# Moving three quarters of the key projections of a decoder layer from ahead of the loop into its first three steps, with the loads put in another order

## The chip, the cores and the metric

One core of one Trainium2 chip. The metric is the device time of one execution in microseconds (us), the median of several runs.

## The reference

A post-norm decoder layer over 32 batches of 128 tokens and 256 channels, all in float32:

```python
x = _layernorm(x + _L0_attn_ref(x, L0_attn_qkv_weights), axis=-1)      # 16 heads of 16, causal softmax
x = _layernorm(x + _L0_xattn_ref(x, ctx_1024, ctx_1024, ...), axis=-1)  # rotary q and k, decay mask, no softmax
x = _layernorm(x + _L0_ffn_ref(x, ...), axis=-1)                        # 8 experts, top 2, and a shared one
```

In the self-attention the keys are taken in an unusual way:

```python
q = jnp.transpose(pre_q, (0, 2, 1, 3)).reshape(-1, S, Dh)
k = jnp.transpose(pre_k, (0, 2, 3, 1)).reshape(-1, S, Dh)
a = jnp.einsum('aib,ajb->aij', q, k) / scale
```

The (channel, token) matrix of each head is read as (token, channel), so a row of k mixes 16 tokens of one channel. The kernel gets this order by a trip of the keys through device memory.

## The kernel before, in words

Five engines run programs of their own and meet on semaphores: TensorE (PE, `@block.tensor`), VectorE (DVE), ScalarE (ACT), GpSimd (POOL) and the DMA queue of SyncE (SP). The attention part is a software pipeline: `step(n)` on each engine handles scores of batch n, turns the probabilities of batch n-1, takes the heads of batch n-2, the cross attention of batches n-3 and n-4, the gate of batch n-5, and projects batch n+1 (`project`, q and v). The later parts (experts on gathered rows, the shared expert, the last norm) follow the loop and are not touched.

The keys go another way. The batches are in four groups of eight (`NG = 4`, `GB = 8`). `project_k(g, j, bank)` makes a quarter of a group's keys, called a tile here: tile i is quarter i % 4 of group i // 4. It is four float32 matmuls, eight in the profile, into one bank of PSUM (line 708). `out_k` (line 1238) copies the tile to SBUF on VectorE and counts `kk_set`. `store_k(g)` (line 445) waits for the group's four copies and stores 1 MB to `k_dram`. For each batch eight loads of 16 KB (line 480) bring its keys back as `kp`, in the order that `scores` (line 756) needs.

Order on TensorE before the loop: tiles 0 to 11 in banks 4 to 7, waits for all small tables and weights, then step -1 with `project(0)` and the first masks. Tiles 12 to 15 are inside: 12 and then 13 and 14 in step 0 behind its scores and its `project(1)`, tile 15 in step 1. The banks are used by others in the loop: 4 for turned probabilities, 5 for heads, 6 for q and v, 7 for the cross attention and the turned x1.

Order on SP before the loop: key weights, the four parts of x of group 0, x of groups 1 to 3 (1 MB each), identity, q and v weights, small loads (`load_small`, line 435: gate weights, biases, 705 KB of tables, the causal mask `tb`, cross attention weights), the store of group 0, then step by step: xT of batch n+2, kp of batch n+1, a store of another group at steps -1, 0 and 1, from step 3 to 6 the weights of the FFN (2.25 MB in the first of them, 1.5 MB in the others), ctx of batch n-2 and x of batch n-1. Each SP step begins with a wait for `project(n+1)` of TensorE (xT of two batches before must be free).

The masks (`lay_mask`, lines 1091 on ScalarE and 1359 on VectorE) write the causal mask of the next batch into the score banks once the exponentials have read them; scores(n+1) waits for all four.

Of the kernel before, what the change touches and what calls it, by code (L numbers as in the profile page):

```python
# [14 lines left out]
P = 128  # L15
# [17 lines left out]
GROUPS = [(lo, 4) for lo in range(0, B - 4, 4)] + [(B - 4, 2), (B - 2, 2)]  # L33
MAX_ORDER = (1, 0, 3, 2)
PADDING = B * S * TOPK
QB = 4
# [55 lines left out]
def decoder_kernel(nc, x, ctx_turned, wqkv, xwq, xwk, xwv, gate_w, gate_b, sw1, sb1, sw2, sb2,  # L92
                   rw1, rb1, rw2, rb2, table_f32, table_bf16, x_turned, x_blocks, out):
    ctx = ExitStack()
    with ctx:
# [196 lines left out]
        kk_set = sem("kk_set")  # L292
        k_stored = [sem("k_stored_first"), sem("k_stored_rest")]

# [110 lines left out]
        def live(t):  # L405
            return 0 <= t < B
# [15 lines left out]
        def _(eng):  # L422
            wqkv_rows = wqkv.rearrange("(c p) n -> p c n", p=P)
            eng.dma_start(wqkv_sb[:, :, D:2 * D], wqkv_rows[:, :, D:2 * D]).then_inc(wk_in, 16)
            for j in range(4):
                eng.dma_start(xTu[0][:, 2 * j:2 * j + 2, :, :, :].rearrange("p u c b i -> p (u c b i)"),
                              x_blocks[0, :, 2 * j:2 * j + 2].rearrange("p u n -> p (u n)")).then_inc(first_in[j], 16)
            for g in range(1, NG):
                eng.dma_start(xTu[g][:, :, :, :, :].rearrange("p u c b i -> p (u c b i)"),
                              x_blocks[g].rearrange("p u n -> p (u n)")).then_inc(xTu_in[g], 16)  # L430
            eng.dma_start(ident, table_f32[:, 0:P]).then_inc(ident_in, 16)
            for n in (0, 2):
                eng.dma_start(wqkv_sb[:, :, n * D:(n + 1) * D], wqkv_rows[:, :, n * D:(n + 1) * D]).then_inc(w_in, 16)

            def load_small():
                eng.dma_start(gate_w_sb[:, :, :], gate_w.rearrange("(c p) n -> p c n", p=P)).then_inc(small_in, 16)
                eng.dma_start(gate_b_sb[:, 0:NE], gate_b.rearrange("(o n) -> o n", o=1).broadcast_to([P, NE])).then_inc(small_in, 16)
                eng.dma_start(sb1_sb[:, :], sb1[0].rearrange("(c p) -> p c", p=P), allow_slow_non_contiguous=True).then_inc(small_in, 16)
                eng.dma_start(sb2_sb[:, :], sb2.broadcast_to([P, D])).then_inc(small_in, 16)
                eng.dma_start(tf[:, P:], table_f32[:, P:]).then_inc(tables_in, 16)  # L440
                eng.dma_start(tb[:, :], table_bf16).then_inc(tables_in, 16)
                for w, src in ((xwq_sb, xwq), (xwk_sb, xwk), (xwv_sb, xwv)):
                    eng.dma_start(w[:, :, :], src.rearrange("(c p) n -> p c n", p=P)).then_inc(xw_in, 16)

            def store_k(g):
                eng.wait_ge(kk_set, g * 4 + 4)
                eng.dma_start(k_dram[g * GB:(g + 1) * GB].rearrange("b i g f -> (b i) (g f)"),
                              kk_of(g)).then_inc(k_stored[min(g, 1)], 16)

            load_small()  # L450
            store_k(0)

# [13 lines left out]
            def step(n):  # L466
                t = n + 2
                if live(t):
                    after(eng, qv_made, t - 1)
                    eng.dma_start(xT[:, t % 2, :, :], x_turned[t]).then_inc(xT_in[t % 2], 16)  # L470
                t = n + 1
                if live(t):
                    after(eng, scored, (t - 1) * 4)
                    if t < 2:
                        eng.wait_ge(consts_set, 2)
                    if t == 0:
                        eng.wait_ge(k_stored[0], 16)
                    for j in range(GB):
                        lo = 16 * j
                        eng.dma_start(kp[lo:lo + DH, t % 2, j % 2, :, :].rearrange("p a u -> p (a u)"),  # L480
                                      k_dram[t, :, j, :]).then_inc(kp_in[t % 2], 16)
                if n in (-1, 0, 1):
                    store_k(n + 2)
                if n == 3:
                    eng.wait_ge(k_stored[1], 16 * (NG - 1))
                if 2 < n <= 2 + NE // 2:
                    if n == 3:
# [3 lines left out]
                    for e in range(2 * (n - 3), 2 * (n - 2)):  # L491
# [11 lines left out]
                if live(t):  # L503
                    after(eng, res1_set, t - 1)
                    eng.dma_start(xn[:, t % 2, :], x[t]).then_inc(xn_in[t % 2], 16)
                if n == B:
                    eng.wait_ge(qv_made, B)
# [196 lines left out]
        def _(eng):  # L704
# [8 lines left out]

            for g in range(NG - 1):
                eng.wait_ge(xTu_in[g] if g else wk_in, 16)
                for j in range(4):
                    if g == 0:
                        eng.wait_ge(first_in[j], 16)
                    else:
                        eng.wait_ge(kk_set, (g - 1) * 4 + j + 1)  # L720
                    project_k(g, j, 4 + j)
            eng.wait_ge(xTu_in[NG - 1], 16)
            eng.wait_ge(ident_in, 16)
            eng.wait_ge(w_in, 32)
            eng.wait_ge(kk_set, 4 * NG - 5)
            eng.wait_ge(tables_in, 32)
            eng.wait_ge(xw_in, 48)
            eng.wait_ge(small_in, 64)
            eng.wait_ge(consts_set, 2)

            def project(t):
# [96 lines left out]

            def step(n):
                if n == 1:  # L830
                    eng.wait_ge(kk_set, 13)
                if live(n - 1):
                    turn_probs(n - 1, 0)
                if n == 2:
                    eng.wait_ge(kk_set, 4 * NG)
                if live(n - 2):
# [3 lines left out]
                if n == 0:  # L840
                    eng.wait_ge(kk_set, 9)
                    project_k(NG - 1, 0, 4)
                if n == 1:
                    eng.wait_ge(kk_set, 14)
                    project_k(NG - 1, 3, 5)
                t = n - 3
# [20 lines left out]
                if live(n - 1):  # L867
                    turn_probs(n - 1, 1)
                t = n - 3
                if live(t):  # L870
# [23 lines left out]
                if live(n - 1):  # L894
                    turn_probs(n - 1, 2)
                t = n - 5
                if live(t):
# [31 lines left out]
                if n == 0:  # L929
                    eng.wait_ge(kk_set, 12)  # L930
                    project_k(NG - 1, 1, 5)
                    project_k(NG - 1, 2, 7)
                for q in groups_at(n, 3):
# [15 lines left out]
                if live(t):  # L949

                    eng.wait_ge(x1_set, t + 1)
                    after(eng, gc_set, n - 4)
# [282 lines left out]
        def _(eng):  # L1235
            def out_k(g, j, bank):
                eng.wait_ge(k_made, g * 4 + j + 1)
                eng.tensor_copy(kk_of(g).rearrange("p (a u) -> p u a", u=NU)[:, 2 * j:2 * j + 2, :],
                                ps[:, bank, :].rearrange("p (u a) -> p u a", u=2)).then_inc(kk_set, 1)

            for g in range(NG - 1):
                for j in range(4):
                    out_k(g, j, 4 + j)
            eng.wait_ge(tables_in, 32)
            eng.wait_ge(consts_set, 2)
            eng.tensor_copy(base[:, :], region_rows).then_inc(base_set, 1)

            eng.tensor_copy(zeros[:, D:PACKET], padding_end).then_inc(zeros_set, 1)

# [111 lines left out]
            def step(n):  # L1361
                t2, t3, t4, t5 = n - 2, n - 3, n - 4, n - 5
                r2, r4 = t2 % 2, t4 % 2
                if live(n):
                    for u in MAX_ORDER[:3]:
# [3 lines left out]
                if n == 0:  # L1369
                    for j, bank in enumerate((4, 5, 7)):  # L1370
                        out_k(NG - 1, j, bank)
                if n == 1:
                    out_k(NG - 1, 3, 5)
                if live(t2):
# [279 lines left out]
```

## Time and profile before

| | us |
|---|---|
| median of 3 runs | 769.59 |
| lowest, highest | 768.74, 775.72 |
| the profiled execution | 775.48 |
| its span | 773.6 |

The span is that from the first to the last instruction in the trace; the rest of the profiled execution's time lies around it. The mean granted TensorE clock of the span is 0.967 of full speed.

### The profile page before, as it was taken

What the parts mean: (1) busy time and instruction counts of PE and PEld (TensorE: products, weight loads), DVE (VectorE), ACT (ScalarE), POOL (GpSimd) and SP (SyncE); (2) the same over time, 40 slices, a digit from 0 to 9 for tenths busy, and PEclk for the clock granted to TensorE, in tenths of its full rate; (3) what the DMA queues carried; (4) which work ended last, traced back from release to release, by engine and by line L of the source; (5) the groups of instructions that cost most, each with busy time, mean ns of one, the idle gap of its engine ahead of it and who ended that gap; (6) DMA issues with size and microseconds to landing.
All of it is one profiled execution on the core that took longest, in us unless ns stands there. A gap on an engine that the chain in (4) does not pass through costs nothing.

```text
span 773.6 us, 19404 instructions
## 1 busy us (share of the span) xinstructions
PE 705.6 (91%) x5464; PEld 533.1 (69%) x5465; DVE 499.1 (65%) x1568; ACT 410.3 (53%) x1167; POOL 319.1 (41%) x451
## 2 busy tenths in 40 slices
PE   6978899999999999999987639999999999999993
PEld 6857788888888888888875315666666666665453
DVE  3555678888988888898866432444444444438985
ACT  0268688888888888888851102333333333312233
POOL 1001233335554554455455542555555555541111
PEclk9999999999999999999999677999999999999998
DMA  8644462213332332333271432422222222229962
GB/s 290 253 145 157 138 223 74 83 57 106 102 97 82 103 109 77 100 101 108 85 228 62 151 124 88 152 83 88 83 87 89 82 89 84 86 61 320 302 215 81
DMA packets 77032, 97.54 MB, mean 126 GB/s; under 512 B 12320, under 2 KB 63264, under 8 KB 75936
## 3 DMA queue, kind: packets, MB, share of 16 engines
q1 hardware_dynamic: 59920, 68.21, 28.0%
q0 software_dynamic: 6816, 19.00, 6.8%
q10 hardware_dynamic: 10224, 9.42, 4.4%
q8 instruction: 39, 0.64, 0.3%
q14 instruction: 33, 0.27, 0.1%
HBM read 60.02 MB, written 36.56 MB: 125 GB/s over the span
## 4 chain that ended last, share of the span: by engine, by line
PE 67%; issue 14%; DVE 5%; SPq 5%; DMA 4%; POOL 2%; ACT 1%; POOLq 0%; ACTq 0%; DVEq 0%
PE ps L990 16%; PE ps L1001 8%; PE ps L777 5%; PE ps L765 4%; PE ps L855 4%; PE ps L742 4%; PE ps L787 4%; PE ps L879 3%; PE ps L745 3%; PE ps L858 3%; PE ps L976 2%; PE ps L983 2%; DMA attn_only<-in_ctx 2%; DVE products L1263 2%; PE ps L865 2%
## 5 line engine op out<-in xcount | busy, mean ns | idle before, releaser
L1079 ACT ACTIVATE prob<-ps,nmax 128x128 f32<-128x128 f32 x512 | 146.8, 378 | 30.2 <-DVE nmax L1253 30.2
L990 PE MATMUL ps<-first_use,xgT 128*128 x284 | 137.3, 607 | 1.3 <-ACT xgT L1184 1.2
L1486 DVE TENSOR_TENSOR hid<-ps,attn_only 128x512 f32<-128x512 f32 x71 | 49.1, 692 | 93.8 <-PE ps L990 93.8
L1184 ACT COPY xgT<-ps 128x256 f32<-128x256 f32 x71 | 26.5, 373 | 133.9 <-PE ps L976 131.7
L1253 DVE TENSOR_REDUCE nmax<-ps 128x4 f32<-128x512 f32 x128 | 82.2, 685 | 22.7 <-PE ps L765 21.0
L671 POOL TENSOR_TENSOR gate_h<-hid,sil 128x256 f32<-128x256 f32 x71 | 50.9, 717 | 100.3 <-DVE result_row L1499 82.7
L1086 ACT COPY pT<-ps 128x512 f32<-128x512 f32 x128 | 76.7, 599 | 19.2 <-PE ps L777 14.5
L621 POOL TENSOR_TENSOR rot<-products 128x128 f32<-128x128 f32 x128 | 61.2, 499 | 60.9 <-DVE products L1263 57.8
L777 PE MATMUL ps<-tf,prob 128*128 128x128 f32 x512 | 78.6, 276 | 5.8 <-ACT pT L1086 5.7
L990 PEld LDWEIGHTS ps<-first_use,xgT 128*128 128x128 f32 x284 | 54.7, 194 | 41.1 <-issue 37.5
L640 POOL DMA_INDIRECT sent<-packets,pos x64 | 63.6, 994 | 37.1 <-PE ps L765 22.8
L674 POOL DMA_INDIRECT back<-yg,result_row x71 | 71.8, 1011 | 13.8 <-issue 12.3
L1001 PE MATMUL ps<-first_use,ghT 128*128 x284 | 74.0, 383 | 0.5 <-ACT ghT L1189 0.5
L777 PEld LDWEIGHTS ps<-tf,prob 128*128 128x128 f32 x512 | 59.3, 141 | 11.7 <-issue 5.4
L795 PE MATMUL ps<-prob,sw_sb 128*128 128x512 f32 x128 | 62.5, 639 | 3.9 <-DMA prob<-x2T_dram 2.7
L976 PEld LDWEIGHTS ps<-tf,xg 128*128 128x128 f32 x142 | 19.1, 144 | 54.9 <-issue 54.2
L1505 DVE TENSOR_TENSOR yg<-ps,attn_only 128x256 f32<-128x256 f32 x71 | 30.2, 425 | 39.3 <-PE ps L1001 36.7
L1001 PEld LDWEIGHTS ps<-first_use,ghT 128*128 128x128 f32 x284 | 48.3, 190 | 4.9 <-issue 0.9
L1263 DVE TENSOR_TENSOR products<-ps,tf 128x256 f32<-128x256 f32 x128 | 46.3, 404 | 6.0 <-PE ps L879 2.0
L795 PEld LDWEIGHTS ps<-prob,sw_sb 128*128 128x128 f32 x128 | 25.5, 203 | 33.4 <-issue 29.2
L653 POOL TENSOR_TENSOR rstd<-mv,neg_half 128x1 f32<-128x1 f32 x32 | 17.7, 552 | 67.5 <-DVE mv L1271 67.5
L1359 DVE CAST ps<-tb 128x512 f32<-128x512 bf16 x62 | 42.0, 682 | 2.1 <-ACT prob L1079 2.1
(135 smaller groups left out, 1390.2 us busy)
## 6 DMA issues: line engine op xcount, KB each, us to landing
xg<-sent ACTq DMA_DIRECT2D x68, 129.5 KB
first_use<-back SPq DMA_DIRECT2D x8, 1024.0 KB, 8.2
k_dram<-first_use SPq DMA_DIRECT2D x4, 1024.0 KB, 4.3
attn_only<-in_x_turned SPq DMA_DIRECT2D x32, 128.0 KB, 2.7
attn_only<-k_dram SPq DMA_DIRECT2D x256, 16.0 KB
attn_only<-in_x SPq DMA_DIRECT2D x32, 128.0 KB, 2.6
attn_only<-in_ctx SPq DMA_DIRECT2D x32, 128.0 KB, 2.6
first_use<-in_L_ffn_rw SPq DMA_DIRECT2D x8, 512.0 KB, 5.0
```

Of the source, the lines that this page charges most:

```text
L621: eng.tensor_tensor(rot[:, t % 2, m + e, :], ra[:, t % 2, m + e, :], rb[:, t % 2, m + 1 - e, :], ALU.add).then_inc(done, 1)
L640: eng.indirect_dma_start(sent, bass.IndirectOffsetOnAxis(ap=pos[:, t, j:j + 1], axis=0), packets[:, t % SLOTS, :], None).then_inc(sent_in[ ...
L671: eng.tensor_tensor(gate_h[:, r, :], hid[:, r, FFN:2 * FFN], sil[:, r, :], ALU.mult).then_inc(gh_set, 1)
L674: eng.indirect_dma_start(back, bass.IndirectOffsetOnAxis(ap=result_row[:, slot:slot + 1], axis=0), yg[:, slot % 2, :], None).then_inc(yg_o ...
L777: mm = eng.transpose(PROBT[:, n * P:(n + 1) * P], prob[:, t % 2, 4 * u + n, :], ident)
L795: mm = eng.matmul(ps[:, bank0 + 2 * f + half, :].rearrange("p (b t) -> p b t", b=QB), sw1_sb[:, c, cols:cols + P], x2T4[:, r, :, c, :], st ...
L990: mm = eng.matmul(ps[:, r, :], xgT[:, r, c, :], rw1_sb[:, bass.ds(e * (DC * 2 * FFN) + c * 2 * FFN, 2 * FFN)], start=(c == 0), stop=(c == ...
L1001: mm = eng.matmul(ps[:, 4 + r, 0:D], ghT[:, r, c, :], rw2_sb[:, bass.ds(e * (FFN // P * D) + c * D, D)], start=(c == 0), stop=(c == FFN // ...
L1079: ins = eng.activation(prob[:, t % 2, 4 * u + n, :], SCORE[u][:, n * P:(n + 1) * P], ACT.Exp, bias=nmax[:, t % 2, 4 * u + n:4 * u + n + 1])
L1086: eng.copy(pT[:, u, :, :].rearrange("p n t -> p (n t)"), PROBT).then_inc(pT_set, 1)
L1253: eng.tensor_reduce(nmax[:, t % 2, 4 * u:4 * u + 4], SCORE[u].rearrange("p (h j) -> p h j", j=P), AX_X, ALU.max, negate=True).then_inc(max ...
L1263: eng.tensor_tensor(into[:, t % 2, m:m + 2, :], source, table[:, m:m + 2, :], ALU.mult).then_inc(done, 1)
```

## The change

Tiles 0 to 3 are projected ahead of the loop and copied there. Tiles 4 to 15 move: 4, 5 and 6 to the head of step 0 ahead of its scores, 7 and 8 behind scores(0), 9 and 10 behind `project(1)`; 11 behind scores(1), 12 and 13 behind the second and third turn of the probabilities in step 1; 14 behind scores(2) and 15 behind the third turn of step 2. `K_BANK` names each tile's bank; a tile waits until the one before it in the same bank has been copied. The copies on VectorE move along, in program order. The base and zeros copies of VectorE move from ahead of the loop to step 1.

The loads have a new order: q and v weights, xT of batches 0 and 1, the mask (with a semaphore of its own) and the identity go in front; then x of group 1, the small loads, x of groups 2 and 3. The store of group 0 is split: batch 0 (16 partitions, 128 KB) and the rest, each with its semaphore; batch 0's kp waits for the first alone. The other stores come at the end of SP's steps 0, 1 and 2 instead of in the middle of -1, 0 and 1, and the FFN weights at steps 4 to 7 instead of 3 to 6. TensorE's waits for tables, cross attention weights and small loads move to the steps that use them.

```diff
+K_BANK = (4, 5, 6, 7, 4, 5, 7, 4, 5, 7, 5, 7, 5, 7, 7, 7)
@@ SP
-            for g in range(1, NG):
+            for n in (0, 2):
+                eng.dma_start(wqkv_sb[:, :, n * D:(n + 1) * D], wqkv_rows[:, :, n * D:(n + 1) * D]).then_inc(w_in, 16)
+            for t in range(2):
+                eng.dma_start(xT[:, t, :, :], x_turned[t]).then_inc(xT_in[t], 16)
+            eng.dma_start(tb[:, :], table_bf16).then_inc(mask_in, 16)
+            eng.dma_start(ident, table_f32[:, 0:P]).then_inc(ident_in, 16)
+
+            def load_blocks(g):
                 eng.dma_start(xTu[g][:, :, :, :, :].rearrange("p u c b i -> p (u c b i)"),
                               x_blocks[g].rearrange("p u n -> p (u n)")).then_inc(xTu_in[g], 16)
-            eng.dma_start(ident, table_f32[:, 0:P]).then_inc(ident_in, 16)
-            for n in (0, 2):
-                eng.dma_start(wqkv_sb[:, :, n * D:(n + 1) * D], wqkv_rows[:, :, n * D:(n + 1) * D]).then_inc(w_in, 16)
...
             def store_k(g):
                 eng.wait_ge(kk_set, g * 4 + 4)
-                eng.dma_start(k_dram[g * GB:(g + 1) * GB].rearrange("b i g f -> (b i) (g f)"),
-                              kk_of(g)).then_inc(k_stored[min(g, 1)], 16)
-
+                rows = k_dram[g * GB:(g + 1) * GB].rearrange("b i g f -> (b i) (g f)")
+                if g == 0:
+                    eng.dma_start(rows[0:DH, :], kk_of(g)[0:DH, :]).then_inc(k_stored[0], 16)
+                    eng.dma_start(rows[DH:P, :], kk_of(g)[DH:P, :]).then_inc(k_stored[1], 16)
+                else:
+                    eng.dma_start(rows, kk_of(g)).then_inc(k_stored[2], 16)
+
+            load_blocks(1)
             load_small()
+            for g in range(2, NG):
+                load_blocks(g)
             store_k(0)
@@ SP, step
-                if live(t):
+                if live(t) and t > 1:
                     after(eng, qv_made, t - 1)
                     eng.dma_start(xT[:, t % 2, :, :], x_turned[t]).then_inc(xT_in[t % 2], 16)
...
-                    if t == 0:
-                        eng.wait_ge(k_stored[0], 16)
+                    if t < 2:
+                        eng.wait_ge(k_stored[t], 16)
...
-                if n in (-1, 0, 1):
-                    store_k(n + 2)
-                if n == 3:
-                    eng.wait_ge(k_stored[1], 16 * (NG - 1))
-                if 2 < n <= 2 + NE // 2:
+                if n == 4:
+                    eng.wait_ge(k_stored[2], 16 * (NG - 1))
+                if 3 < n <= 3 + NE // 2:
...
+                if n in (0, 1, 2):
+                    store_k(n + 1)
@@ TensorE
-            for g in range(NG - 1):
-                ...
-                    project_k(g, j, 4 + j)
+            def project_ks(first, end):
+
+                for i in range(first, end):
+                    if i == 0:
+                        eng.wait_ge(wk_in, 16)
+                    if i < 4:
+                        eng.wait_ge(first_in[i], 16)
+                    elif i % 4 == 0:
+                        eng.wait_ge(xTu_in[i // 4], 16)
+                    if K_BANK[i] in K_BANK[:i]:
+                        eng.wait_ge(kk_set, i - K_BANK[:i][::-1].index(K_BANK[i]))
+                    project_k(i // 4, i % 4, K_BANK[i])
+
+            project_ks(0, 4)
             eng.wait_ge(w_in, 32)
+            eng.wait_ge(mask_in, 16)
             eng.wait_ge(consts_set, 2)
+            eng.wait_ge(kk_set, 3)
@@ VectorE, step
+                if n == 0:
+                    out_ks(4, 7)
+                    eng.wait_ge(mask_in, 16)
+                    eng.wait_ge(consts_set, 2)
                 if live(n):
                     for u in MAX_ORDER[:3]:
                         maxes(n, u)
                     if n < 2:
                         maxes(n, MAX_ORDER[3])
                 if n == 0:
-                    for j, bank in enumerate((4, 5, 7)):
-                        out_k(NG - 1, j, bank)
+                    out_ks(7, 11)
                 if n == 1:
-                    out_k(NG - 1, 3, 5)
+                    out_ks(11, 14)
+                    eng.wait_ge(tables_in, 16)
+                    eng.tensor_copy(base[:, :], region_rows).then_inc(base_set, 1)
+                    eng.tensor_copy(zeros[:, D:PACKET], padding_end).then_inc(zeros_set, 1)
+                if n == 2:
+                    out_ks(14, 16)
```

## Rows read from the trace of the kernel before

**Rows 1.** The page, busy time of TensorE and of VectorE over the span.

```profile
PE 705.6 (91%) x5464; PEld 533.1 (69%) x5465; DVE 499.1 (65%) x1568; ACT 410.3 (53%) x1167; POOL 319.1 (41%) x451
```

**Rows 2.** Chain of waits up to scores(1): start us, us, what.

```profile
18.63 8.60 DMA k_dram<-first_use
...
30.46 1.62 DMA attn_only<-k_dram
...
32.22 1.17 PE ps L765 x32
33.39 1.92 PE ps L708 x8
35.32 0.89 PE ps L742 x8
36.21 0.87 PE ps L745 x4
37.07 3.47 PE ps L708 x16
...
40.56 1.08 DVE first_use L1238
41.65 1.19 DVE ps L1359 x2
```

**Rows 3.** Chain of waits, steps 1 and 3: start us, us, what.

```profile
43.08 1.70 PE ps L765 x32
44.78 3.02 PE ps L708 x8
47.80 0.45 PE ps L777 x4
...
48.28 0.59 ACT pT L1086
48.87 0.14 issue
...
54.23 1.18 PE ps L765 x32
...
71.78 7.96 DMA attn_only<-in_ctx
```

**Rows 4.** DMA view of the first 32 us: GB/s in 40 slices of 0.8 us.

```profile
GB/s 0 0 55 365 156 146 246 315 379 410 417 420 461 399 451 410 410 412 337 365 179 123 193 315 338 390 378 433 424 424 387 278 129 47 8 30 32 39 40 188
```

**Rows 5.** Source view of the stores of keys (line 447), 0 to 80 us.

```profile
DMA to landing us min/median/max: 4.2/4.3/8.6
```

**Rows 6.** Windows: stretch, us, busy of each engine, granted clock, DMA share, GB/s.

```profile
44.00:46.00 2.00, 2.00 (x19) 1.59 (x15) 1.21 (x3) 0.48 (x2) 0.00 (x0) 0.50 0.13 33
46.00:48.00 2.00, 2.00 (x10) 1.62 (x9) 1.44 (x4) 1.70 (x7) 0.00 (x0) 0.76 0.00 0
...
65.95:76.53 10.58, 9.50 (x123) 8.34 (x119) 7.16 (x17) 9.20 (x28) 2.41 (x5) 1.00 0.68 217
76.53:91.38 14.85, 12.33 (x129) 10.50 (x125) 8.44 (x23) 9.40 (x28) 3.03 (x6) 0.89 0.56 184
91.38:102.50 11.12, 10.92 (x136) 9.79 (x132) 8.75 (x25) 9.58 (x29) 3.76 (x7) 1.00 0.59 189
```

**Rows 7.** Timeline of TensorE: start us, us, instructions [idle before them and its releaser].

```profile
43.08 1.70 PE L765 MATMUL ps<-attn_only 32*128 32x128 f32 x32 [2.12 <-DVE ps L1359]
...
58.92 0.63 PE L777 MATMUL ps<-tf,prob 128*128 128x128 f32 x4 [2.34 <-ACT pT L1086]
...
79.79 1.16 PE L855 MATMUL ps<-attn_only 128*128 128x128 f32 x8 [2.09 <-DMA attn_only<-in_ctx]
```

**Rows 8.** Timeline of VectorE, columns as in rows 7.

```profile
14.82 1.08 DVE L1238 COPY first_use<-ps 128x512 f32<-128x512 f32 x1 [0.65 <-PE ps L708]
...
57.20 0.25 DVE L1376 RECIPROCAL rden<-ps 128x16 f32<-128x16 f32 x1
...
59.16 0.69 DVE L1253 TENSOR_REDUCE nmax<-ps 128x4 f32<-128x512 f32 x1
```

More of the change, by code:

```diff
@@ L292, in decoder_kernel @@
         kk_set = sem("kk_set")
-        k_stored = [sem("k_stored_first"), sem("k_stored_rest")]
+        k_stored = [sem("k_stored_batch"), sem("k_stored_group"), sem("k_stored_rest")]
+        mask_in = sem("mask_in")
         xT_in = [sem("xT_in0"), sem("xT_in1")]
@@ L481, in step @@
                                       k_dram[t, :, j, :]).then_inc(kp_in[t % 2], 16)
-                if n in (-1, 0, 1):
-                    store_k(n + 2)
-                if n == 3:
-                    eng.wait_ge(k_stored[1], 16 * (NG - 1))
-                if 2 < n <= 2 + NE // 2:
-                    if n == 3:
+                if n == 4:
+                    eng.wait_ge(k_stored[2], 16 * (NG - 1))
+                if 3 < n <= 3 + NE // 2:
+                    if n == 4:
                         eng.dma_start(sw1_sb[:, :, :], sw1[0].rearrange("(c p) n -> p c n", p=P)).then_inc(ffn_in, 16)
                         eng.dma_start(sw2_sb[:, :, :], sw2[0].rearrange("(c p) n -> p c n", p=P)).then_inc(ffn_in, 16)
-                    for e in range(2 * (n - 3), 2 * (n - 2)):
+                    for e in range(2 * (n - 4), 2 * (n - 3)):
                         lo = e * DC * 2 * FFN
@@ L712, in project_k @@
                 mm.then_inc(k_made, 1)
-            for g in range(NG - 1):
[L715 to L720, printed above, removed]
-                    project_k(g, j, 4 + j)
-            eng.wait_ge(xTu_in[NG - 1], 16)
-            eng.wait_ge(ident_in, 16)
+            def project_ks(first, end):
[10 more added lines that the diff above has]
+            project_ks(0, 4)
             eng.wait_ge(w_in, 32)
[L725 to L728, printed above, removed]
+            eng.wait_ge(mask_in, 16)
             eng.wait_ge(consts_set, 2)
+            eng.wait_ge(kk_set, 3)
             def project(t):
@@ L829, in step @@
             def step(n):
+                if n == 0:
+                    project_ks(4, 7)
                 if n == 1:
-                    eng.wait_ge(kk_set, 13)
+                    eng.wait_ge(ident_in, 16)
+                    eng.wait_ge(kk_set, 8)
+                if n == 3:
+                    eng.wait_ge(tables_in, 16)
+                    eng.wait_ge(xw_in, 48)
+                if n == 5:
+                    eng.wait_ge(small_in, 64)
                 if live(n - 1):
@@ L834, in step @@
                 if n == 2:
-                    eng.wait_ge(kk_set, 4 * NG)
+                    eng.wait_ge(kk_set, 13)
                 if live(n - 2):
@@ L840, in step @@
                 if n == 0:
-                    eng.wait_ge(kk_set, 9)
-                    project_k(NG - 1, 0, 4)
+                    project_ks(7, 9)
                 if n == 1:
-                    eng.wait_ge(kk_set, 14)
-                    project_k(NG - 1, 3, 5)
+                    project_ks(11, 12)
+                if n == 2:
+                    project_ks(14, 15)
                 t = n - 3
@@ L868, in step @@
                     turn_probs(n - 1, 1)
+                if n == 1:
+                    project_ks(12, 13)
                 t = n - 3
@@ L895, in step @@
                     turn_probs(n - 1, 2)
+                if n == 1:
+                    project_ks(13, 14)
+                if n == 2:
+                    project_ks(15, 16)
                 t = n - 5
@@ L929, in step @@
                 if n == 0:
-                    eng.wait_ge(kk_set, 12)
-                    project_k(NG - 1, 1, 5)
-                    project_k(NG - 1, 2, 7)
+                    project_ks(9, 11)
                 for q in groups_at(n, 3):
@@ L951, in step @@
                     eng.wait_ge(x1_set, t + 1)
+                    if n == 2:
+                        eng.wait_ge(kk_set, 4 * NG)
                     after(eng, gc_set, n - 4)
@@ L1235, in _, with out_ks @@
         def _(eng):
[L1236 to L1248, printed above, removed]
+            def out_ks(first, end):
+                for i in range(first, end):
+                    eng.wait_ge(k_made, i + 1)
+                    eng.tensor_copy(kk_of(i // 4).rearrange("p (a u) -> p u a", u=NU)[:, i % 4 * 2:i % 4 * 2 + 2, :],
+                                    ps[:, K_BANK[i], :].rearrange("p (u a) -> p u a", u=2)).then_inc(kk_set, 1)
+            out_ks(0, 4)
             def maxes(t, u):
@@ L1363, in step @@
                 r2, r4 = t2 % 2, t4 % 2
+                if n == 0:
+                    out_ks(4, 7)
+                    eng.wait_ge(mask_in, 16)
+                    eng.wait_ge(consts_set, 2)
                 if live(n):
@@ L1369, in step @@
                 if n == 0:
-                    for j, bank in enumerate((4, 5, 7)):
-                        out_k(NG - 1, j, bank)
+                    out_ks(7, 11)
                 if n == 1:
-                    out_k(NG - 1, 3, 5)
+                    out_ks(11, 14)
+                    eng.wait_ge(tables_in, 16)
+                    eng.tensor_copy(base[:, :], region_rows).then_inc(base_set, 1)
+                    eng.tensor_copy(zeros[:, D:PACKET], padding_end).then_inc(zeros_set, 1)
+                if n == 2:
+                    out_ks(14, 16)
                 if live(t2):
```

1 line of the change is left out of this document (removed).

## The prediction

> **What bounds the kernel now.** The page comes first: TensorE is busy for 91% of the span and no other engine for more than 65% [rows 1]. So TensorE's order of work sets the time, and an edit is worth what it takes from or adds to TensorE's path. The change acts only on the first steps, so the next view is the chain of waits over the first 60 us. It runs through the DMA queue, not through TensorE, until 32.22: store of the first group's keys (lands 27.23), eight loads of batch 0's padded keys, and only then scores(0) at 32.22 [rows 2]. All twelve projections that stand ahead of the loop lie beside that DMA work and cost nothing. From 32.22 on the chain is TensorE with short hand-overs. I use the start of scores(n) (line 765) as the clock of the steps: 32.22, 43.08, 54.23 [rows 2, 3], then 65.95, 76.53, 91.38, 102.5 [rows 6]. The third view is the DMA rate by slices of 0.8 us [rows 4], for what a transfer is queued behind. The fourth is the granted clock [rows 6]: it is 0.50 in 44 to 46, after TensorE had stood still for 2.1 us [rows 7]. The fifth is the order of TensorE and VectorE in step 2 [rows 7, 8].
>
> **The start.** The store of group 0 is still issued after every load. Bytes ahead of it, counted from the shapes: 6.83 MB before, 7.09 MB after, since the two xT loads now stand ahead of it. Summing the slices of [rows 4], 6.83 MB have passed at 22.4 us and the store's 1.05 MB at 24.6; it lands at 27.23, 2.6 later. After: 7.09 MB have passed at 23.1, batch 0's 0.13 MB at 23.4, so it lands between 25.3 and 26.0; I take 25.6, a gain of 1.6. From landing to scores(0) was 32.22 - 27.23 = 4.99 (eight issues, the last one's landing of 1.62 [rows 2]) and is the same again. Scores(0) then starts at about 30.6. Bounds: no gain, if the small store lands with its sibling; and 3.0, if it lands 1.2 sooner still. The keys themselves are no limit: the fourth copy is done at 15.9 [rows 8]. The Trainium skill, "DMA: Bandwidth & Descriptors", Rules for kernel authors, says of two transfers to disjoint partition halves "Don't bother — they serialize". By that rule the split would be worth nothing in bytes; what I count is only that the first part's own semaphore fires earlier, and the slices agree that bytes go in order (8.60 us for the queued store against a median of 4.3 [rows 2, 5]).
>
> **What moves into the loop.** Before, 12 of 16 tiles (a tile is one project_k) come ahead of the loop and 4 inside steps 0 and 1. After, 4 come ahead, 3 (tiles 4 to 6) between the first masks and scores(0), where TensorE waits for the keys anyway, and 9 inside steps 0 to 2 behind a scores. That is five tiles more on the path side. A warm tile is 3.47 / 2 = 1.73 us [rows 2], so 8.7 us more work. The cover is what TensorE idles in these steps.
>
> Ahead of scores(0): TensorE works on 7 tiles, project(0) and the masks and ends near 22, then waits over 8 us. Before, it came to scores(0) after under 1 us of idling at full clock. The nearest row for a start after a wait is scores(1): 1.70 instead of 1.17 for the scores and 3.02 instead of 1.92 for the tile behind it, at a granted clock of 0.50, which is the 1.2 GHz level [rows 2, 3, 6]. The Trainium skill, "TensorE: Matmul & The Clock Gate", Part 1, also has TensorE fall to the lower of two clocks when idle; a wait of 8 us would then be answered by these same cold rows.
>
> Step 0: scores 1.70, tile 7 cold 3.02, tile 8 1.73, project(1) 0.89 + 0.87 = 1.76, tiles 9 and 10 3.47, then as before VectorE's copy of the last tile 1.08, two masks 1.19, hand-overs 0.27: 14.2. Before it was 10.86. So **+3.4**. Bounds: +1.7 if TensorE were warm, the bare extra tile; +6.5 if it stayed cold for the whole step (further tiles at 3.02, project(1) at twice its time less the overlap).
>
> Step 1: scores(1) follows again a 2.1 us wait for VectorE's masks, so 1.70 and 3.02 stay. Tiles 12 and 13 now stand between the turns of the probabilities, where TensorE waited 0.02 + 0.59 + 0.14 = 0.75 for ScalarE twice [rows 3]. So 2 x (1.73 - 0.75) less the slower turns = 1.6: the step goes from 11.15 to 12.7, **+1.6**. VectorE's four maxima, three copies and its base and zeros copies end before scores(2) needs its masks; ScalarE's last pT, exponentials, mask and q copy end 0.5 before the TensorE work does. Nobody else is late.
>
> Step 2: tile 14 falls into the idle time ahead of the turn at 58.92 [rows 7] (2.3 us long, so it is free). Tile 15 stands between the third and the fourth turn. VectorE does its copy, by program order, before the reciprocal, res1, the last maximum and x1. Before, the reciprocal began at 57.20, 2.97 after scores(2). After, tile 15 ends 4.69 + 0.44 + 1.73 = 6.86 after scores(2), its copy at 7.96, and the maximum 1.96 later [rows 8] at 9.9. Then ScalarE's four exponentials (1.15), x1T, mask and q copy end at about 13.2, against the 11.7 of before. TensorE has nothing to do from about 9.1 to 11.2 (2.1 us, waiting for x1), so comes out cold, and its transposes, turns and weigh end at about 14.1. I take 14.1 against 11.7: **+2.3**, bound +1.5 if it stays warm. The slow rows after scores(1) span 4.7 us [rows 3]; the same stretch here reaches into step 3: **+1.0**, or 0.
>
> Queues: SP now waits for kk_set 8, 12 and 16 at the end of its steps 0 to 2, in front of xT and kp of the next step. It gets them at 36.5, about 50.7 and s2 + 8; the next entry waits for project(1), (2) and (3), which end later each time. So the stores cost nothing there. POOL's zeros for the idle rows go out near 55 instead of 30.5; no load that is soon due stands behind.
>
> Step 5: the weights of the FFN are issued one step later, so the wait for ctx moves from step 4 to step 5. There it was 79.79 - 77.70 = 2.09 plus a cold stretch; step 4 took 14.85 against 11.12 of step 5, an excess of 3.7 [rows 6, 7]. The ctx issued behind 2.25 MB landed 7.96 after its issue at 71.78 [rows 3], 13.8 after scores(3). Steps 4 and later are 11.1 long instead of step 3's 10.58, so the same landing leaves a wait of 13.8 - 12.3 = 1.5. **-1.0**; bounds -2.2 (0.6 less wait and no cold stretch) and 0.
>
> **Sum** on the profiled execution of 775.5 (span 773.6 and 1.9 around it): -1.6 + 3.4 + 1.6 + 2.3 + 1.0 - 1.0 = +5.7, so 781.2 there. That execution lies 5.9 above the median of 769.6, inside the spread of the three runs (768.7 to 775.7); the difference carries over: **775.3**. From scores(6) on nothing differs.
>
> **Rivals.** (a) *The clock stays up*, because tiles fill TensorE's gaps. Deciding place: scores(0) and the tiles behind it at 1.17 and under 2. Step 0 then +1.7, step 1 -0.2 (1.70 and 3.02 become 1.17 and 1.73), step 2 +1.5, step 3 nothing, step 5 -2.2, start -1.6: -0.8, **768.8**, not slower. For it: idle stretches of 0.77 and 0.95 left the clock alone. Against: 2.1 us didn't, and the new wait is over 8. 0.12.
> (b) *The small store overtakes the loads.* Its place is the queue: if it lands about 2.7 after its issue instead of behind 7 MB, and SP's long issues go with the lighter queue, scores(0) starts near 23.6, -8.6 instead of -1.6; the sum is -1.3, **768.3**. It decides if k_stored fires before about 20. Against it is the 8.60 of [rows 2]. 0.05.
> (c) *TensorE stays cold through step 0 and part of step 1.* The wait before it is four times any seen here. Step 0 +6.5, one more tile of step 1 cold +1.3: +10, about **779.7**, slower by over 1%. 0.22.
> (d) The forecast, 0.61.
>
> **From this to the numbers.** About 1% (7.7 us) is what this kernel's measurement tells from no change, given the spread above. The forecast's own bounds run from about 771 to 779. The range takes in (a) and most of (c): 768.5 to 779.5, with some 2 in 10 outside. Slower by over 1% means above 777.3: (c) and a little of (d), 0.24. Faster by over 1% means below 761.9, which no case reaches: 0.02. The rest is 0.74.
>
> **What the changed profile would show.** Scores(0) at 30 to 31; 1.70 and about 3.0 for it and the tile behind; 14.2, 12.7 and 14.1 from scores to scores; tile 15's copy directly ahead of the reciprocal in step 2; the wait for ctx in step 5, near 1.5; 11.1 for step 4. It would be wrong if the first store lands at another time than 25 to 26, or if the clock answers the long wait otherwise.

## The result, and the profile after

The changed kernel takes 775.16 us (median of 20 runs), the kernel before 770.31 (20 runs). The ratio is 1.0067, 95% interval [1.0045, 1.0088]: 5.2 us slower, between 3.5 and 6.8. The ratio leaves out three slow runs of the changed kernel (one of them took 934.7 us at a granted clock of 0.834), so it does not quite match the two medians, which are 4.9 us apart. The forecast was 775.3. A second series of the same kernel gave 1.0070 [1.0029, 1.0110] (the run after_again).

The chain of waits of the profiled execution (span 772.9) up to step 5: start us, us, what. It answers to [rows 2, 3].

```profile
15.55 11.17 DMA k_dram<-first_use
...
29.92 1.62 DMA attn_only<-k_dram
31.54 0.14 issue
31.68 2.09 PE ps L779 x32
33.77 4.80 PE ps L720 x16
38.57 0.89 PE ps L756 x8
39.46 0.86 PE ps L759 x4
40.32 3.47 PE ps L720 x16
43.79 0.02 issue
43.81 1.08 DVE first_use L1267
44.90 1.19 DVE ps L1381 x2
46.08 0.28 issue
46.36 2.09 PE ps L779 x32
48.45 2.56 PE ps L720 x8
...
58.99 1.18 PE ps L779 x32
...
89.10 7.41 DMA attn_only<-in_ctx
```

The windows of the steps, from scores to scores; it answers to [rows 6]. Columns: stretch, us, busy time of PE, PEld, DVE, ACT and POOL, granted clock, DMA share, GB/s.

```profile
31.68:46.36 14.68, 12.53 (x81) 10.80 (x81) 8.00 (x10) 6.59 (x21) 0.00 (x0) 0.85 0.34 115
46.36:58.92 12.56, 12.56 (x117) 10.91 (x117) 6.99 (x11) 7.68 (x23) 1.15 (x1) 0.87 0.24 92
58.92:72.00 13.08, 10.34 (x119) 8.69 (x115) 7.97 (x15) 8.78 (x26) 0.58 (x1) 1.00 0.64 201
72.00:82.57 10.57, 9.50 (x122) 8.33 (x118) 7.16 (x17) 9.23 (x28) 2.41 (x5) 1.00 0.16 45
82.57:93.60 11.03, 10.71 (x129) 9.12 (x125) 8.45 (x23) 9.30 (x28) 3.01 (x6) 1.00 0.61 191
93.60:106.60 13.00, 11.01 (x134) 9.82 (x131) 8.78 (x25) 9.56 (x29) 3.77 (x7) 1.00 0.71 225
```

The timeline of TensorE at its longest waits, which answers to [rows 7], and that of VectorE in step 2, which answers to [rows 8]:

```profile
31.68 2.09 PE L779 MATMUL ps<-attn_only 32*128 32x128 f32 x32 [9.47 <-DMA attn_only<-k_dram]
...
70.18 0.44 PE L982 MATMUL ps<-tf,x 128*128 128x128 f32 x2 [1.95 <-DVE x L1438]
...
96.56 1.16 PE L877 MATMUL ps<-attn_only 128*128 128x128 f32 x8 [1.78 <-DMA attn_only<-in_ctx]
```

```profile
66.07 1.09 DVE L1267 COPY first_use<-ps 128x512 f32<-128x512 f32 x1 [2.92 <-PE ps L720]
67.00 0.22 DVE L1406 RECIPROCAL rden<-ps 128x16 f32<-128x16 f32 x1
...
68.93 0.69 DVE L1275 TENSOR_REDUCE nmax<-ps 128x4 f32<-128x512 f32 x1
```

Line 779 is scores, 720 a tile, 877 the first matmul on ctx, 1267 a tile's copy. The reader is to see: scores(0) starts only 0.54 us sooner (31.68), after a wait of 9.47; step 0 is 3.8 longer than before, step 1 1.5, step 2 1.3, step 3 the same, step 4 3.8 shorter (the wait for ctx has left it) and step 5 1.9 longer (it has come here). Scores(8) starts at 129.03, before at 125.26: +3.8. From scores(8) to scores(31) every profile of this study shows 257.2 to 257.8, so what the change does is over at scores(8), and I use that mark for each kernel. The spans of the two profiled executions (773.6 and 772.9) do not show the difference: that of before lost 2.6 us more between scores(31) and the first expert tile, and 2 more in the experts, in work that the change does not touch. The mark has its own spread: a second profile of before has it at 129.66, a second one of the changed kernel at 130.99 (the runs before_again and after_again), so one profile against one shows where time goes, and not the total.

| start of scores, us | 0 | 1 | 2 | 3 | 4 | 5 | 6 | 8 |
|---|---|---|---|---|---|---|---|---|
| before | 32.22 | 43.08 | 54.16 | 65.95 | 76.53 | 91.38 | 102.49 | 125.26 |
| after | 31.68 | 46.36 | 58.92 | 72.00 | 82.57 | 93.60 | 106.60 | 129.03 |
| after_again | 31.80 | 47.20 | 59.84 | 73.80 | 85.04 | 96.06 | 108.52 | 130.99 |
| before_again | 36.86 | 50.59 | 60.46 | 72.24 | 82.82 | 95.18 | 106.30 | 129.66 |

### The profile page after: what moved, and what is told of

Its sections match the earlier page's. It is cut to its first block, busy times and chain, and to the rows that moved or that the text cites. A ratio compares the mean times of both kernels' runs of the same rounds, so it can differ in the third digit from the quotient of the medians.

```text
span 772.9 us, 19407 instructions
## 1 busy us (share of the span) xinstructions
PE 700.9 (91%) x5464; PEld 530.8 (69%) x5465; DVE 498.8 (65%) x1568; ACT 410.4 (53%) x1167; POOL 318.6 (41%) x451
## 4 chain that ended last, share of the span: by engine, by line
PE 70%; issue 14%; DVE 5%; POOL 4%; DMA 4%; SPq 1%; ACT 1%; POOLq 0%; ACTq 0%; DVEq 0%
PE ps L1018 16%; PE ps L1029 8%; PE ps L791 5%; PE ps L779 5%; PE ps L877 4%; PE ps L801 4%; PE ps L756 4%; PE ps L880 3%; PE ps L903 3%; PE ps L759 3%; PE ps L720 3%; PE ps L1004 2%; POOL sent L652 2%; PE ps L1011 2%; DVE products L1285 2%
## 5 line engine op out<-in xcount | busy, mean ns | idle before, releaser
L1018 PE MATMUL ps<-first_use,xgT 128*128 x284 | 135.6, 600 | 1.5 <-ACT xgT L1212 1.5
L779 PE MATMUL ps<-attn_only 32*128 32x128 f32 x1024 | 39.4, 292 | 11.6 <-DMA attn_only<-k_dram 9.5
L665 POOL TENSOR_TENSOR rstd<-mv,neg_half 128x1 f32<-128x1 f32 x32 | 17.6, 550 | 68.4 <-DVE mv L1293 68.4
```

Of the source, the lines that this page charges most:

```text
L779: mm = eng.matmul(SCORE[u][:, n * P:(n + 1) * P].rearrange("p (d u) -> p d u", u=NU), qT[32 * u:32 * u + 32, t % 2, c, :], kp[32 * u:32 * ...
L1018: mm = eng.matmul(ps[:, r, :], xgT[:, r, c, :], rw1_sb[:, bass.ds(e * (DC * 2 * FFN) + c * 2 * FFN, 2 * FFN)], start=(c == 0), stop=(c == ...
```

## The experiments

All ratios are against the kernel before, run on the same chip beside them; one profile each. The median of the kernel before was 770.31 to 773.52 us in the different series, so ratios, and not times, are to be compared between experiments. Where the start of scores(8) is given as sooner or later, it is against the first profile of the kernel named.

**1. Loads alone** (loads_only): the kernel before with the new load order and the split store; tiles, stores of groups 1 to 3 and FFN weights as before.

> The kernel before with the new order of loads and the split store, and the tiles where they were. Theory (the moved tiles cost, the loads do not): scores(0) starts at 31.7 to 32.0 instead of 32.22, the steps are those of before (10.9, 11.1, 11.8), the time is within 0.2% of before. Rival (the order of loads costs by itself, as group 2's x now lands late and holds tiles 8 to 11 and with them project(0)): scores(0) after 33, 0.2 to 0.5% slower. Rival of the other sign (the loads bring what was to be had and only the tiles hide it): 30.6 and 0.2% faster.

Measured: 771.69 us, ratio 0.9992 [0.9972, 1.0013]. In its profile scores(0) starts at 33.30: the x of group 2 lands late (its load ends the wait of TensorE at 23.5) and tiles 8 to 11, project(0) and the masks follow it. Steps 0 and 1 are 10.86 and 11.14. Step 2 is 10.12 instead of 11.79, and step 4 is 17.60 instead of 14.85, with a wait of 3.88 for ctx, so the theory's "steps of before" did not hold there, and scores(8) is at 127.51 (+2.3). So the place of scores(0) is what the first rival said, its price in the time is not seen, and the loads alone neither pay nor gain: the 0.67% comes with the rest of the change, the tiles above all.

**2. Tiles alone** (tiles_only): the changed kernel with the loads in the old order and the store in one piece.

> The changed kernel with the loads in the order of before and group 0's store in one piece: xT of batches 0 and 1 and the causal mask then stand behind the small loads and the store in the queue. Theory: project(0) waits for xT, which lands near 28, and tiles 4 to 6 come behind it, so scores(0) starts at 35 to 37 instead of 31.7 and the time is 4 to 5 us above the changed kernel (1.1 to 1.3% above before). Rival (only the number of tiles behind scores(0) matters): scores(0) at 32.2, the time that of the changed kernel plus 0.5.

Measured: 780.86 us, ratio 1.0095 [1.0056, 1.0134]. Scores(0) at 37.59, steps 12.59, 12.68, 13.48. TensorE's timeline (start us, us, work, idle before):

```profile
28.26 2.05 PE L749 MATMUL ps<-attn_only 128*128 128x128 f32 x8 [12.90 <-DMA attn_only<-in_x_turned]
...
32.32 5.34 PE L713 MATMUL ps<-attn_only,prob 128*128 128x256 f32 x24
37.59 1.17 PE L772 MATMUL ps<-attn_only 32*128 32x128 f32 x32
```

Project(0) waits 12.9 us for xT, and the three tiles behind it, which cost nothing in the change, are now ahead of scores(0). TensorE comes warm to it, so step 0 is 2.1 shorter than in the change. Scores(0) is later than the 35 to 37 expected, but the time rose less than expected (1.1 to 1.3%), and its interval overlaps that of the change. In the traces the two halves of the change belong together: with the old loads scores(0) comes 5.9 later, and the new loads without the new places bring it 1.1 later than before. That either of these delays costs time by itself is not shown.

**3. The split** (one_store): group 0's store in one piece in the changed kernel.

```diff
-                    eng.dma_start(rows[0:DH, :], kk_of(g)[0:DH, :]).then_inc(k_stored[0], 16)
-                    eng.dma_start(rows[DH:P, :], kk_of(g)[DH:P, :]).then_inc(k_stored[1], 16)
+                    eng.dma_start(rows, kk_of(g)).then_inc(k_stored[0], 16)
```

> The changed kernel with group 0's keys stored in one piece again, batch 0's loads waiting for the whole. If the small store lands ahead of its sibling, the store now lands near 27.5 and scores(0) starts 0.8 us later, at 32.5. If the split is worth nothing, because the engines that carry the small store finish no sooner than the whole queue, the landing stays at 26.7 and scores(0) at 31.7. The rest is unchanged, and the time moves by at most 0.1%.

Measured: 780.65 us, ratio 1.0129 [1.0075, 1.0183] (four runs), more than the 0.1% expected; the interval overlaps that of the change. The store, issued at 16.82, takes 12.01 and lands at 28.8, scores(0) at 33.90, 2.2 later. The split store landed at 26.7 (15.55 + 11.17), 26.3 in experiment 1 and 26.9 in experiment 4. So the split is worth about 2 us at scores(0), and not the 0.8 that I expected. The second part, of 896 KB, lands at 28.8 in the changed kernel, where the unsplit store lands: the split lets the small part be done sooner and does not hasten the rest. And the new load order makes the whole store land later than in the old one (28.8 against 27.23 [rows 2]; 28.16 in before_again), where 0.26 MB more ahead of it would make 0.6 us. DMA rates in slices of 0.8 us over the first 32 us, first of this run, then of the changed kernel:

```profile
GB/s 0 0 79 351 131 123 335 289 302 311 379 389 407 427 399 274 223 256 271 265 306 384 427 402 424 431 381 451 430 410 369 143 154 133 113 10 0 26 36 41
GB/s 0 0 115 334 104 210 251 320 324 328 376 378 380 424 399 267 183 330 347 331 345 405 449 390 469 371 453 420 410 471 297 123 51 61 67 53 28 33 45 164
```

Until 24.8 the rate of this run is near 400; then it is 113 to 154 for four slices. In the changed kernel it is 123 and then 51 to 67. Before, it was 278 in the slice from 24.8 and then 129 and 47 [rows 4]. So the end of the queue runs slowly, for some 3 us in the new order, which a sum over mean rates does not foresee. In the changed kernel all but some 0.1 MB of the 8.14 MB up to the end of the store had passed when the small part landed at 26.7, so it is this slow end, and not the time of 0.9 MB at full rate, that the small part is spared. Why the end is slow was not tried.

**4. A busy TensorE** (kept_busy): 20 matmuls in the wait ahead of scores(0).

```diff
                 if n == 0:
                     project_ks(4, 7)
+                    eng.wait_ge(q_set, 1)
+                    eng.wait_ge(v_set, 1)
+                    for _ in range(20):
+                        eng.matmul(QV[:, 0:D], xTu[1][:, 0, 0, :, :].rearrange("p b i -> p (b i)"), wqkv_sb[:, 0, D:2 * D],
+                                   start=True, stop=True)
```

> The changed kernel with 20 matmuls more on TensorE in the wait ahead of scores(0), into the free bank of q and v, their results never read; no work of the layer is left out. They fill about 8.6 of the 9.5 us. Theory (the clock): scores(0) takes 1.17 instead of 2.09 and the tile behind it 1.9 instead of 3.0, so step 0 goes from 14.7 to 12.6 to 12.8 and the time falls by 2 us (0.25%). Rival (step 0 is long only by the number of tiles and VectorE's hand-over): step 0 stays within 0.3 of 14.7.

Measured: 775.08 us, ratio 1.0027 [0.9998, 1.0056]. The chain of waits:

```profile
23.81 8.63 PE ps L849 x40
32.44 1.10 PE ps L779 x32
33.55 3.65 PE ps L720 x16
...
44.99 1.50 PE ps L779 x32
```

The windows of scores(0), first of the changed kernel, then of this run (the granted clock is the third number from the end):

```profile
31.68:33.77 2.09, 2.09 (x33) 1.86 (x33) 0.00 (x0) 0.00 (x0) 0.00 (x0) 0.50 0.30 86
32.37:34.20 1.83, 1.83 (x36) 1.66 (x36) 0.49 (x1) 0.00 (x0) 0.00 (x0) 1.00 0.14 35
```

Scores(0) 1.17 by the timeline instead of 2.09, two tiles 3.65 instead of 4.80, step 0 12.62 instead of 14.68: the clock is worth 2.06 in step 0, as expected. The ratio moves the same way (1.0067 to 1.0027), but the intervals overlap, so the gain in the time is not shown. In this one profile the gain is given back (scores(8) at 128.99): TensorE began 0.4 later and its added work ran 0.7 past the place of scores(0), and step 2 is 13.97, cold behind the wait for x1.

**5. The shift of the FFN weights alone** (ffn_later): the kernel before, weights at steps 4 to 7 of SP.

> The kernel before with nothing changed but the FFN weights issued at steps 4 to 7 of the DMA queue instead of 3 to 6. Theory: step 4 falls from 14.85 to 11.1, step 5 rises from 11.1 to 13.0 (wait for ctx of 1.8 and full clock behind it), 1.9 us gained in all (0.25% faster). Rival (the saving after the change came from its longer steps, not from the shift): step 5 takes the whole 14.8, no gain.

Measured: 770.51 us, ratio 0.9983 [0.9954, 1.0011]. Step 4 is 11.03, step 5 12.43 with a wait for ctx of 1.25; the two are 23.46 instead of 25.96, so 2.5 less. Step 2 was 12.74 in this profile, at a granted clock of 0.73, against 11.79, so scores(8) came at 123.67, 1.6 sooner. The shift saves without longer steps in front; the time agrees in sign, but its interval takes in no change.

**6. ctx ahead of the weights** (ctx_first in the changed kernel, before_ctx_first in the kernel before): SP's loads of ctx and x stand ahead of the FFN weights within a step.

> The changed kernel with ctx and x of the two coming batches issued ahead of the FFN weights in each step of the DMA queue instead of behind them. Theory (the weights ahead of ctx make the wait of step 5): step 5 falls from 13.0 to 11.1, all else the same, 1.9 us (0.25%) faster than the changed kernel. Rival (the transfer is late because the queue is full of the keys of the coming batch, whatever stands ahead): step 5 stays near 13.

> The kernel before with ctx and x issued ahead of the FFN weights in each step of the DMA queue, nothing else. Theory (step 4 of before is long by the wait for ctx and the cold stretch behind it): step 4 falls from 14.9 to 11.1, 3.7 us (0.5%) faster than before. Rival (another transfer or engine is late next): less than half of it.

Measured: 775.46 us, 1.0050 [1.0021, 1.0080], and 769.73 us, 0.9972 [0.9929, 1.0015]. No wait for ctx is left in either profile. Step 5 is 11.12 in the one, step 4 is 11.03 in the other, and scores(8) comes at 126.79 (-2.2) and 121.30 (-4.0). The wait is made by the weights ahead of it; neither gain is clear in the time by itself. Not all else stayed the same in the changed kernel: scores(1) came warm (1.17) and step 1 was 11.00, step 3 was 11.78.

**7. The copy of tile 15** (late_copy): VectorE copies it behind x1.

```diff
                 if n == 2:
-                    out_ks(14, 16)
+                    out_ks(14, 15)
@@ behind the tensor_scalar that writes x1
+                if n == 2:
+                    out_ks(15, 16)
```

> The changed kernel with VectorE's copy of tile 15 moved from ahead of the reciprocal of step 2 to behind its x1. Theory (the copy holds VectorE's chain to x1): step 2 falls from 13.1 to 11.0 to 11.8, 1.3 to 2 us less. Rival (step 2 is bound by TensorE's and ScalarE's work with the two tiles in it): step 2 stays at 13, and the copy only ends later.

Measured: 777.92 us, ratio 1.0055 [1.0024, 1.0086]. Its windows of steps 2, 4 and 5, and TensorE's timeline in step 5:

```profile
59.15:70.06 10.91, 10.12 (x119) 8.76 (x115) 7.91 (x15) 8.83 (x26) 0.58 (x1) 1.00 0.64 203
80.64:91.66 11.02, 10.70 (x128) 9.11 (x124) 8.44 (x23) 9.29 (x28) 3.03 (x6) 1.00 0.62 182
91.66:108.70 17.04, 13.69 (x134) 12.21 (x130) 8.74 (x25) 9.68 (x29) 3.76 (x7) 0.80 0.55 178
```

```profile
95.93 2.07 PE L877 MATMUL ps<-attn_only 128*128 128x128 f32 x8 [3.09 <-DMA attn_only<-in_ctx]
97.80 1.91 PE L880 MATMUL ps<-attn_only 128*128 128x256 f32 x4
```

Step 2 falls from 13.08 to 10.91, as the theory said: the copy held the chain to x1. But step 5 takes 17.04: TensorE waits 3.09 for ctx and then runs at about half its pace (2.07 for eight matmuls that take 1.16 warm). Step 5 is 4.0 longer than in the changed kernel, more than the 2.2 saved. Ctx was issued 1.7 sooner (87.44 against 89.10) but took 8.44 instead of 7.41 to land, so most of the early start went into the wait, and the cold stretch behind it took the rest. Scores(8) comes at 131.13, 2.1 later.

**8. Batch 0's store ahead of the bulk** (store_first).

```diff
             load_blocks(1)
-            load_small()
-            for g in range(2, NG):
-                load_blocks(g)
-            store_k(0)
+            eng.wait_ge(kk_set, 4)
+            eng.dma_start(keys_of(0)[0:DH, :], kk_of(0)[0:DH, :]).then_inc(k_stored[0], 16)
+            load_blocks(2)
...
+                if n == -1:
+                    eng.dma_start(keys_of(0)[DH:P, :], kk_of(0)[DH:P, :]).then_inc(k_stored[1], 16)
+                    load_blocks(3)
+                if n == 0:
+                    load_small()
```

> The changed kernel with batch 0's store ahead of x of groups 2 and 3 and of all small loads and tables: x of group 1, store of batch 0, x of group 2, batch 0's eight key loads, the rest of group 0's store, x of group 3, batch 1's key loads, and only then the small loads. Theory (what holds scores(0) is the 7 MB ahead of the store): the store lands within 4 us of its issue at 15.6 to 17, scores(0) starts at 23.5 to 25 instead of 31.7, without a cold TensorE ahead of it, so step 0 is 12.6 and scores(1) comes 9 to 10 us sooner; the time is 1.2% below that of the changed kernel and 0.5% below that of the kernel before. Rival (the store is held by its own slow shape, 16 partitions): it takes 9 us or more from issue to landing again and nothing is won. Rival (the loads put behind are missed later): scores(0) is early, but a tile or a table is waited for in steps 0 to 3 and half or more is given back.

Measured: 772.30 us, ratio 0.9996 [0.9962, 1.0030]. The chain of waits:

```profile
16.35 2.63 DMA k_dram<-first_use
...
24.10 1.17 PE ps L781 x32
25.27 3.65 PE ps L722 x16
...
36.69 1.37 PE ps L781 x32
```

The same small store lands in 2.63 instead of 11.17, scores(0) starts at 24.10, step 0 is 12.59 and scores(1) comes 9.7 sooner than in the changed kernel. So the queue ahead of the store held scores(0), not its shape. The queue had in fact run empty: SP waits for the keys before it issues more, and the DMA rate is 0 from 13.6 to 16.8. By scores(8) only 6.2 is left: step 2 is 13.92 (cold behind x1's wait), step 3 11.30, step 5 14.88 with a wait of 2.05 for ctx. It makes up the loss of the change, 0.7% of the 1.2% expected; it does not beat the kernel before.

**9. The three together** (all_three).

> The three edits of the other runs together (store of batch 0 first, ctx ahead of the weights, copy of tile 15 behind x1). If they act in separate places, their gains add: 13 us below the changed kernel, about 1.1% below the kernel before. If an early start is only moved into later waits, less than two thirds of the sum.

Measured: 763.06 us (761.37 to 764.38), ratio 0.9886 [0.9853, 0.9918]. The windows of steps 0 to 5:

```profile
22.71:35.30 12.59, 10.47 (x80) 9.17 (x81) 7.91 (x10) 6.52 (x21) 0.00 (x0) 1.00 0.56 163
35.30:47.94 12.64, 12.64 (x116) 10.81 (x117) 6.99 (x11) 7.68 (x23) 1.15 (x1) 0.86 0.89 332
47.94:58.84 10.90, 10.12 (x118) 8.76 (x114) 7.92 (x15) 8.82 (x26) 0.58 (x1) 1.00 0.64 200
58.84:69.43 10.59, 9.52 (x123) 8.35 (x119) 7.16 (x17) 9.21 (x28) 2.41 (x5) 1.00 0.31 90
69.43:80.45 11.02, 10.71 (x129) 9.12 (x125) 8.44 (x23) 9.29 (x28) 3.03 (x6) 1.00 0.64 187
80.45:91.56 11.11, 10.91 (x134) 9.78 (x130) 8.74 (x25) 9.57 (x29) 3.76 (x7) 1.00 0.79 253
```

Scores(8) at 114.08, 15.0 sooner than in the changed kernel. This is the version that beats both, by 8.8 us (6.3 to 11.4) against before, 1.1% as expected. Of the 15.0, 1.4 are an earlier start in this profile against that of experiment 8 (scores(0) at 22.71 against 24.10; the first wait for x ended 1.3 sooner). Apart, the three moved the ratio by -0.0071, -0.0017 and -0.0012, in sum -0.0100; together by -0.0181. With intervals of 0.003 to each side of every ratio, that they add to more than their sum is only just clear in the time. The traces say how it can be: experiment 8 lost in step 2 and in the wait for ctx, experiment 7 in the wait for ctx, and here step 2 is 10.90 and no such wait is left. Whether the moved tiles are needed for this gain is not shown: the kernel before with its own store put first was not tried.

**10. Each kernel once more** (after_again, before_again).

> The changed kernel once more, to see how far one profiled execution speaks for others. If the steps are fixed by the order of work, steps 0 and 1 are again 14.7 and 12.6 within 0.2; where a transfer is waited for (scores(0), step 5), it may differ by 1 to 4 us.

> The kernel before once more, for the same reason: steps 0 and 1 again 10.9 and 11.1 within 0.2, step 4 between 13 and 17.6.

Measured: after_again 777.59 us, ratio 1.0070 [1.0029, 1.0110]; before_again, one run, 779.69. Step 1 of after_again is 12.64 as said, step 0 is 15.40, 0.7 off; step 2 13.96, step 5 12.46. In before_again steps 0 and 1 are 13.73 and 9.87, neither of them as said, step 4 12.36. Its scores(0) started at 36.86:

```profile
36.86 2.09 PE L765 MATMUL ps<-attn_only 32*128 32x128 f32 x32 [5.43 <-DMA attn_only<-k_dram]
```

Batch 0's keys landed 5.33 after their last issue instead of 1.62. GpSimd's 906 KB of zeros were issued at 29.66 in it, ahead of that last key load (SP issued the eight from 28.23 to 32.2); in the first profile of before they went out at 30.47, with the key loads issued from 27.30 to 30.88. So an execution of the kernel before can lose 4.6 us at scores(0), probably to these zeros; it was not tried apart. In the change they go out at 57.2.

## Why the prediction was right, point by point

The time (775.16 for 775.3) and the sign are those of the forecast. Four terms were off by 1 us each in the first profile, one up and three down, so the median agrees better than the reasons do; in the second profile of the same kernel steps 2 and 3 are nearer to the forecast. The agreement to 0.1 us is luck: the forecast added 5.7 to a median of three runs, 769.6, and the medians of twenty are 770.3 and 4.9 more. What the runs bear out is the way the time moved and that it moved by about 5 us.

- *The start*, -1.6 forecast, -0.5 measured (31.68 and 31.80 for 30.6). Mis-sized: the landing of the small store, 26.7 instead of 25.6. The step "it lands at 27.23, 2.6 later" failed. I also summed [rows 4] wrongly there: the store's bytes have passed at 25.1, not 24.6, so the landing was 2.1 later. In the changed kernel 7.22 MB have passed at 23.0 by the same sum, and the small store landed 3.7 later. Experiment 3 shows the slow end of the queue; without the split the start would have been a loss. Rival (b), the store overtaking, did not happen in the change; experiment 8 shows what an early landing is worth (-7.6 at scores(0)), and that it takes another place in the queue. The sum of rival (b) was short of a term: with the early store scores(0) comes warm, so step 0 is 12.59, +1.7 and not the +3.4 that the sum kept.
- *Step 0*, +3.4 forecast, +3.8 and +4.5 measured. Mis-sized by the scores after the long wait, 2.09 where I took the 1.70 of a shorter one, and in after_again by two tiles of 5.54 in place of 4.80. The clock is the larger part: experiment 4 takes 2.1 away, the extra tile's 1.73 stays. Rival (a) needs a warm start that the change does not have; rival (c), a step cold to its end, did not come: project(1) was at full pace again (0.89). The bound of +6.5 that (c) used does not follow from its own terms: three further tiles at 3.02 and project(1) at twice its time add 5.6 to the 3.4, about +9, from which only an overlap without a size is taken.
- *Step 1*, +1.6 forecast (12.7), +1.5 measured (12.56 and 12.64). Right: by the two chains, a tile of 1.73 stands where a gap of 0.75 was, twice; scores(1) and the tile behind it took 2.09 and 2.56 where I took 1.70 and 3.02, nearly the same sum. In ctx_first it was 11.00, as scores(1) came warm there, which is what rival (a) had for it.
- *Step 2*, +2.3 forecast (14.1), +1.3 measured. The mechanism is as told, tile 15's copy directly ahead of the reciprocal and TensorE waiting 1.95 for x1; experiment 7 shows it. The clock was a guess: in this profile it stayed up (granted 1.00), and the step is then below even the warm bound of +1.5; in after_again (13.96) and in experiments 4 and 8 (13.97, 13.92) it did not (granted 0.93 in each of the three).
- *Step 3*, +1.0 forecast, 0.0 measured, for the same reason; after_again has 11.24, +0.7.
- *Steps 4 and 5*, -1.0 forecast, -1.9 measured, -2.5 in after_again. The wait of 1.78 came close to the 1.5, but no cold stretch followed (1.16 for the matmuls on ctx). Experiments 5 and 6 show that the shift of the weights and the wait behind them account for it.
- *Sum to scores(8)*: +5.7 forecast, +3.8 in one profile and +5.7 in the other, against the first profile of before. Against its second (129.66) they are -0.6 and +1.3, so single profiles don't settle the sum; the time does, with +5.2 (3.5 to 6.8).

## What to carry to other kernels

Work that stands in the shadow of a load is free; moved into a loop that one engine bounds, it costs its full time less the gaps that it fills, and here also 2.1 us for the slower clock behind the long wait that it left. A thing that the loop's start waits for gains by its place in the transfer queue, not by being cut small at the queue's end: the same 128 KB store took 11.17 us behind 7 MB and 2.63 in a queue that had run empty; cut small at the queue's end it gained 2.1. A gain in front of a wait for a late transfer can be lost in it (experiment 7), so take such waits away first. Judge small edits by marks inside the trace as well as by the time, but from more than one profile: two of one kernel differed by 2.0 and by 4.4 us at the same mark.

## What the runs showed of the hardware

- After a wait of 9.47 us the 32 small matmuls of scores took 2.09 instead of 1.17, at a granted clock of 0.50, the lower level (1.2 of 2.4 GHz). They took 2.09 as well behind waits of 5.43 (before_again) and of 7.87, 8.76, 8.86 and 10.44 us (ctx_first, late_copy, after_again, one_store). After waits of about 2 us both were seen, in the same place of the same program: scores(1) took 1.70 and 1.17 in the two profiles of before, 2.09 and 1.48 in those of the change. In step 2 of the changed kernel, behind a wait of 1.95 for x1, weigh and scores(3) took 1.08 and 1.17 by the first profile; by TensorE's timeline of after_again, behind the same wait:

```profile
71.10 0.44 PE L982 MATMUL ps<-tf,x 128*128 128x128 f32 x2 [1.95 <-DVE x L1438]
...
71.93 1.94 PE L801 MATMUL ps<-pT,va 128*32 128x128 f32 x32
73.80 1.83 PE L779 MATMUL ps<-attn_only 32*128 32x128 f32 x32
```

  So a sum over cold and warm durations can't be exact to less than 1 us for each such wait.
- The time that ctx took behind the same 2.25 MB differed between kernels and executions: waits of 1.0 to 3.9 us for it, and steps of 12.2 to 17.6 us. What sets it was not found.
